# A four-layer cross-attention and expert kernel: first query weight in four transfers, idle products ahead, and two query products moved up

## The reference, cut to what matters

```
h = layernorm(x)                                    # 1024 tokens x 512
# layer 0: 32 query heads of 128, 4 key/value heads; keys from context and h (128 per sequence)
q = h @ Wq0;  k, v = concat(ctx, h) @ Wk0, Wv0
x = x + softmax(q k^T / sqrt(128)) v @ Wo0
x = x + experts0(layernorm(x))                      # dense 512x512 + top 2 of 28 low-rank experts
# layer 1: 32 query heads of 128, 8 key/value heads; keys from the context alone (64 per sequence)
q = rmsnorm(h @ Wq1.T);  k = rmsnorm(ctx @ Wk1.T);  v = ctx @ Wv1.T
x = x + softmax(q k^T / sqrt(128) + mask) v @ Wo1.T
x = x + experts1(layernorm(x))                      # top 2 of 8
# layers 2 and 3: another attention, experts, and a clustered linear part; untouched here
```

## Time and profile before

| | |
|---|---|
| median of three runs | 1587.48 us |
| the profiled execution's own time | 1586.25 us |
| span in the trace, first to last instruction | 1584.4 us |
| TensorE (PE) busy | 1502.9 us, 95% |
| VectorE (DVE) busy | 1010.4 us, 64% |
| ScalarE (ACT) busy | 820.3 us, 52% |
| GpSimd (POOL) busy | 380.0 us, 24% |
| mean granted TensorE clock | 0.984 |

### The profile page before, as it was taken

The page is one execution under the profiler, slowest core; times in us unless marked ns, Lnnn a source line. Parts: engine busy times, 40 slices in busy tenths (PEclk is TensorE's granted clock), DMA queues, the critical chain, the costliest instruction groups (busy, mean ns, idle before and its releaser), DMA issues.

```text
span 1584.4 us, 27734 instructions
## 1 busy us (share of the span) xinstructions
PE 1502.9 (95%) x9626; PEld 1321.7 (83%) x9626; DVE 1010.4 (64%) x2475; ACT 820.3 (52%) x2862; POOL 380.0 (24%) x388
## 2 busy tenths in 40 slices
PE   6999999999999998989999999999999998779996
PEld 5899999999999987778888888888888887667775
DVE  6556556655665568765566656666565677688775
ACT  4455445645555455346565655555555652464542
POOL 4102010210111011133232323323232321543420
PEclk9999999999999999999999999999999998899998
DMA  5100100100011001010101010101010001111001
GB/s 182 59 28 28 41 28 28 58 10 28 28 54 41 28 13 41 28 40 28 41 28 41 28 41 28 50 19 67 3 66 32 5 8 54 43 49 40 21 14 57
DMA packets 14191, 60.21 MB, mean 38 GB/s; under 512 B 2036, under 2 KB 3444, under 8 KB 8936
## 3 DMA queue, kind: packets, MB, share of 16 engines
q1 hardware_dynamic: 14056, 58.46, 10.4%
HBM read 56.36 MB, written 2.10 MB: 37 GB/s over the span
## 4 chain that ended last, share of the span: by engine, by line
PE 58%; issue 27%; DVE 8%; POOL 4%; ACT 2%; DMA 0%; POOLq 0%; DVEq 0%; SPq 0%; ACTq 0%
PE psY L865 15%; PE psQ L786 10%; PE psKV L808 8%; PE psSO L755 3%; PE psSO L852 2%; PE psQ L771 2%; PE psTP L818 2%; PE psSO L756 2%; PE psTP L771 1%; POOL wo L483 1%; PE psTP L836 1%; POOL wkv L483 1%; PE psQ L716 1%; PE psKV L729 1%; PE psQ L1130 1%
## 5 line engine op out<-in xcount | busy, mean ns | idle before, releaser
L865 PE MATMUL psY<-wo,oT 128*128 128x512 f32 x1536 | 384.9, 399 | 1.8 <-DVE oT L1699 1.2
L865 PEld LDWEIGHTS psY<-wo,oT 128*128 128x128 f32 x1536 | 278.4, 188 | 66.0 <-POOL wo L483 2.2
L483 POOL TENSOR_TENSOR wo<-stage_o,wo 128x512 fp32r<-128x512 f32 (+2 forms) x71 | 91.3, 1316 | 323.0 <-ACT wo L1261 323.0
L1261 ACT ACTIVATE pT<-psTP 128x512 fp32r<-128x512 f32 (+1 forms) x128 | 62.9, 491 | 168.3 <-PE psTP L836 168.3
L589 POOL TENSOR_TENSOR rms<-ms_eps,minus_half 128x5 f32<-128x5 f32 x64 | 74.7, 1167 | 284.7 <-DVE ms_eps L1862 283.9
L1335 ACT ACTIVATE prob<-s_sb,neg_mx 128x64 f32<-128x64 f32 x256 | 86.0, 337 | 104.9 <-DVE neg_mx L1849 104.9
L1338 ACT ACTIVATE prob<-wide,neg_mx 128x128 f32<-128x128 f32 x256 | 99.8, 391 | 73.9 <-DVE neg_mx L1849 73.7
L1699 DVE TENSOR_TENSOR pT<-psTP,pT 128x512 fp32r<-128x512 f32 (+1 forms) x128 | 71.2, 557 | 78.6 <-ACT pT L1261 77.7
L1699 DVE TENSOR_TENSOR v<-psKV,v 128x128 fp32r<-128x128 f32 x64 | 18.7, 292 | 147.1 <-ACT v L1261 147.1
L808 PEld LDWEIGHTS psKV<-wkv,arena 128*128 128x128 f32 x768 | 99.5, 190 | 12.8 <-issue 6.3
L771 PE MATMUL psQ<-hT,wq 128*128 128x256 f32 x768 | 101.5, 288 | 7.7 <-DVE hT L1699 6.4
(11 more groups left out here) (296 smaller groups left out, 3377.2 us busy)
## 6 DMA issues: line engine op xcount, KB each, us to landing
stage_q<-in_wq SPq DMA_DIRECT2D x16, 1024.0 KB, 5.3
stage_o<-in_wo SPq DMA_DIRECT2D x16, 1024.0 KB, 4.8
stage_kv<-in_wkv SPq DMA_DIRECT2D x12, 512.0 KB, 3.6
stage_q<-in_ctx SPq DMA_DIRECT2D x16, 256.0 KB, 2.7
stage_o<-in_ctxT SPq DMA_DIRECT2D x2, 1024.0 KB, 7.3
stage_q<-in_base SPq DMA_DIRECT2D x2, 1024.0 KB, 5.8
out<-x_res SPq DMA_DIRECT2D x8, 256.0 KB, 2.3
x_res<-in_x SPq DMA_DIRECT2D x1, 1536.0 KB, 14.0
```

The lines of the kernel that those rows point to most:

```text
L483: g.tensor_tensor(dst[LO], stage, dst[HI].bitcast(f32), ALU.subtract).then_inc(ld[done or what + "_lo"], 1)
L865: m = mm(psY[:], oT[:, ol, h, :], wo[:, wl, h, :], start=h == 0 and i == 0, stop=h == HQ - 1 and i == 2)
L1261: copy = lambda o, i: nc.scalar.activation(o, i, ACT.Copy)
```

## The change

The first query weight comes in four transfers of 256 KB, each with its own semaphore (`slot0` to `slot3`, which also take over for the later context transfers); SP then waits for the second tile of x before it issues the context, the key weight and the rest. ScalarE and DVE take the slices as they come: three high slices, the tile 0, the fourth slice, tile 1. PE runs ten products of the identity with itself before the first transposes, one between them and five after them; nobody reads their result. In the first attention the high part of the first output weight moves from step 2 to step 1, behind the high part of step 1's keys, and POOL's low part of it moves behind the last `ln_rstd(0, n)`. In the second attention the query products of steps 1 and 2 are made whole at the end of steps 0 and 1, ahead of the query transposes there; that of step 1 is written to psY in place of psQ. `high_wkv` at the last step of a head group moves ahead of the exponentials and `oT_hi`.

```diff
@@ def of banks
+    def q_bank(st):
+        return psY if st.t == 1 else psQ
@@ sync
-        load_wq(io["wq0"][0], 0)
+        for k in range(KT):
+            sp.dma_start(stage_q[:, k], io["wq0"][0][:, k]).then_inc(ld[f"slot{k}"], 16)
+        sp.wait_ge(ld["x1"], 16)
         sp.dma_start(stage_o[:], io["ctxT"][0]).then_inc(ld["ctx_in"], 16)
@@ gpsimd
             if n == 5:
                 low_ctx(1)
-            if n == 6:
-                low_wo(0)
+        low_wo(0)
@@ tensor
             def q_proj(st, first, last):
-                if first == 0:
-                    need(pe, s["q_read"], st.t)
+                if first == 0 and st.t > 1:
+                    pe.wait_ge(s["q_read"], 1 if st.t == 2 else st.t)
...
-                        m = mm(by_eight(psQ[:]), lat(xl, k, n), wq_slice(st.div(NT) + a.wq0, wl, k),
+                        m = mm(by_eight(q_bank(st)[:]), lat(xl, k, n), wq_slice(st.div(NT) + a.wq0, wl, k),
...
                 if a.rms:
-                    if t.exists:
+                    if t.exists and t.t not in (1, 2):
                         q_proj(t, 0, 2)
                     if t2.exists:
                         p_transpose(t2)
                     if t.exists:
-                        q_proj(t, 2, 4)
+                        if t.t not in (1, 2):
+                            q_proj(t, 2, 4)
                         kv_proj(t)
...
                 if t.exists and a.rms:
+                    if t.t < 2:
+                        q_proj(t.back(-1), 0, 4)
                     q_transpose(t)
                     k_transpose(t)
...
+        def idle_products(count):
+            for _ in range(count):
+                mm(psKV[:, 0:P], ident[:], ident[:], start=True, stop=True)
+
         pe.wait_ge(setup["const"], 3)
-        for n in range(2):
-            ln_transpose(0, n, lambda: None)
+        idle_products(10)
+        ln_transpose(0, 0, lambda: None)
+        idle_products(1)
+        ln_transpose(0, 1, lambda: None)
+        idle_products(5)
@@ scalar, attention
                 if a.kv_new(t):
                     kv_read(t)
+                if a.rms and t.res(8) == 7 and t.exists:
+                    if t.static and t.t == STEPS - 1:
+                        high_wkv(13, 144)
+                    else:
+                        high_wkv(t.div(8) + 6)
...
-                if a.rms and t.res(8) == 7 and t.exists:
-                    act.wait_ge(s["kv"], a.kv_n(t) + 1)
-                    if t.static and t.t == STEPS - 1:
-                        high_wkv(13, 144)
-                    else:
-                        high_wkv(t.div(8) + 6)
+                if not a.rms and t.static and t.t == 1:
+                    kT_hi(t)
+                    high_wo(0)
...
-                if t.res(8) == 2 and not (t.static and t.t >= STEPS):
+                if t.res(8) == 2 and not (t.static and t.t >= STEPS) and (a.rms or t.t > 2):
...
-                    if a.kv_new(t):
+                    if a.kv_new(t) and (a.rms or t.t != 1):
                         kT_hi(t)
@@ scalar, start
-        high_wq(0)
+        for k in range(3):
+            first_wq(k)
         ln_hi(0, 0)
+        first_wq(3)
         ln_hi(0, 1)
@@ vector, start
-        low_wq(0)
+        low_wq(0, 2)
         ln_lo(0, 0)
+        low_wq(0, 3)
         ln_lo(0, 1)
         low_ctx(0)
```

More of the change, by code:

```diff
@@ L453, in _ @@
         for n in range(3):
-            sp.dma_start(stage_q[:, n], io["ctx"][:, n]).then_inc(ld[f"c{n}"], 16)
+            sp.dma_start(stage_q[:, n], io["ctx"][:, n]).then_inc(ld[f"slot{n}"], 16)
         sp.wait_ge(N3["w"], 1)
@@ L462, in _ @@
             sp.wait_ge(N3["f_lo"], n - 2)
-            sp.dma_start(stage_q[:, n % 3], io["ctx"][:, n]).then_inc(ld[f"c{n % 3}"], 16)
+            sp.dma_start(stage_q[:, n % 3], io["ctx"][:, n]).then_inc(ld[f"slot{n % 3}"], 16)
         sp.wait_ge(N3["q_tr"], NT)
@@ L1270, in high, with first_wq @@
             copy(dst, stage).then_inc(ld[what + "_hi"], 1)
+        def first_wq(k):
+            act.wait_ge(ld[f"slot{k}"], 16)
+            copy(wq[:, HI, k], stage_q[:, k]).then_inc(ld["wq_hi"], 1)
         def high_wq(load):
             for k in range(KT):
-                high("wq", wq[:, HI, k], stage_q[:, k], (load + 1) * 16)
+                high("wq", wq[:, HI, k], stage_q[:, k], load * 16)
         def high_wq1(load, k):
-            high("wq", wq_slice(load, HI, k), by_eight(stage_q[:, k]), (load + 1) * 16)
+            high("wq", wq_slice(load, HI, k), by_eight(stage_q[:, k]), load * 16)
         def high_wo(load, n=KT):
@@ L1502, in ctx_exp @@
         def ctx_exp(n):
-            act.wait_ge(ld[f"c{n % 4}"], (n // 4 + 1) * 16)
+            act.wait_ge(ld[f"slot{n % 4}"], (n // 4 + 2) * 16)
             nc.scalar.activation(wide[:], stage_q[:, n % 4], ACT.Square,
@@ L1711, in link, with low_wq @@
             dve.wait_ge(chain, mark(instruction))
-        def low_wq(load, stage=stage_q):
-            for k in range(2, KT):
+        def low_wq(load, *slices):
+            for k in slices or (2, 3):
                 dve.wait_ge(ld["wq_hi"], load * 4 + (k + 1))
-                sub_hi(wq[:, LO, k], stage[:, k], wq[:, HI, k]).then_inc(ld["wq_lo_v"], 1)
+                sub_hi(wq[:, LO, k], stage_q[:, k], wq[:, HI, k]).then_inc(ld["wq_lo_v"], 1)
         def ln_stats(ln, n):
@@ L1869, in qk_normalise @@
                 four = lambda t: t[:].rearrange("p (h c) -> p h c", h=HQ)
-                V.tensor_tensor(four(q_sb), four(psQ), rms[:, n, 0:HQ].unsqueeze(2).to_broadcast([P, HQ, HD]),
+                V.tensor_tensor(four(q_sb), four(q_bank(st)), rms[:, n, 0:HQ].unsqueeze(2).to_broadcast([P, HQ, HD]),
                                 ALU.mult).then_inc(s["q_read"], 1)
@@ L2057, in ctx_max @@
         def ctx_max(n):
-            dve.wait_ge(ld[f"c{n % 4}"], (n // 4 + 1) * 16)
+            dve.wait_ge(ld[f"slot{n % 4}"], (n // 4 + 2) * 16)
             V.tensor_reduce(small[:, 8 + n % 2:9 + n % 2], stage_q[:, n % 4], AX.X, ALU.max,
```

6 lines of the change are left out of this document (3 added, 3 removed).

## The result

The changed kernel takes 1570.69 us, the median of 4 runs (1569.39 to 1574.28); the kernel before took 1586.82 us beside it (4 runs, 1582.82 to 1587.54). The ratio is 0.9907, interval 0.9884 to 0.9931: about 15 us faster. The profiled execution took 1570.53 us with a span of 1568.7 us, against 1586.25 and 1584.4. So its own time fell by 15.7 us, where 10.5 were forecast.

What follows compares the result with a forecast made beforehand. TensorE, busy 95% of the span, was taken as the bound, through its waits and half-clock stretches after them. Terms 3.4 + 5.2 + 2.7 - 0.8 = 10.5 us off 1586.25 gave 1575.8 us; range 1569.5 to 1582.

Steps and rivals of the forecast that it cites:

- part 1: Last step of a head group: key weight split before the exponentials removes seven key-product waits, 3.4 us; bounds 0 and 3.4.
- part 2: Start of second attention: earlier query products bring the third query transpose 5.2 us sooner; bounds 1.9 and 6.9 us.
- part 4: Kernel start: first query product 3.2 us sooner, but 0.7 gained and 1.5 lost to clock, -0.8 us; bounds -3.5 and +1.2.
- part 3: First attention, output weight split a step earlier: 1.21 us wait and 1.51 us slow key product go, 2.7 us.
- I take the whole 3.4 us: Key weight split: all seven listed waits of 0.49 us counted as gain, 3.4 us, also the upper bound.
- so I let this loss stand: Second attention, after the third query transpose: half-clock loss of 1.7 us stays, because the wait ahead of it stays.
- The 1.2 that I gave for that case: Output weight split: if the clock falls nevertheless, only 1.2 us of gain is left.
- The landing of the rest of x: Kernel start: same bytes in the queue, so landing stays at 17.1 us; statistics start at best 1.2 us sooner.
- Rival 1: More half-clock stretches go: second attention's third 1.7, start's loss 1.5, later layers 1.7; 15.4 us gain, 1570.9 us; chance 0.15.
- Rival 2: Waits change place: low-keys waits lower the clock in second attention, start costs 3.5 us; 4.5 us gain, 1581.8 us; chance 0.16.
- rivals 3: Only the seven key-weight waits go, 3.4 us, other gains given back; 1582.9 us, within measurement; chance 0.09.
- rival 4: Slower: later layers drop the granted clock in new places; ten further losses make 17 us, 1592.8 us; chance 0.03.

Runs made afterwards that it cites:

- two other traces: Kernel before with one part each: output weight split a step earlier alone, 1582.69 us; start alone (four transfers, idle products, order of slices), 1586.91 us.
- The four kernels with single parts: Kernel before with one part each: key weight split sooner, ratio 0.9974; two query products moved up, 0.9967; output weight earlier, 0.998; start, 1.0008.
- six groups in the right places: Changed kernel plus idle products in six waits: before tiles 2 and 3, third hidden transpose, last layer's first attention step, three in the third layer; 1565.45 us.
- two in wrong ones: Changed kernel with 12 idle products before tiles 2 and 3, plus 7 in the first layer's attention and 9 before the second hidden transpose; 1575.45 us.
- the fifth trace: Kernel before with only the query products of steps 1 and 2 of the second attention moved up, first weight in one transfer; 1580.17 us.

## Why the prediction was right or wrong

The forecast, 1575.8 us, was 5.1 us too high; the direction and the range, 1569.5 to 1582, held. The 5.2 us of the profiled pair that the sum lacks are 1.6 in part 1, 1.5 in part 2, 1.0 in part 4 and 1.3 in stages that no part touches (1.7 less the 0.3 and 0.2 the other way), less 0.1 in part 3. Of these, the 1.3 and 1.0 of part 2's 1.5 are a matter of the execution, as the table shows; that they fell this way is luck. The forecast said 3.4 for part 1 and -0.8 for part 4, and these two were mis-sized.

**Part 1** was right in its mechanism. ScalarE's split came ahead of the exponentials, POOL started 0.08 us after the probabilities were ready (755.50 against 755.00 + 0.42), and all seven waits went. Mis-sized was the term "I take the whole 3.4 us", and its upper bound as well: it measured 5.0. The listed idle time of a wait is not its price. The busy column shows the rest: in this stage TensorE's idle time fell by 3.4 us (4.12 to 0.71), and its busy time by 1.6 (571.49 to 569.92) with no instruction less. The fall over the whole stage, 5.0 us, is measured from starts to starts; its split is less firm, since the profile models the ends of products. My reading of it, which no run isolates: a product that ends in a wait has its last result's way out (its drain) uncovered, and that is counted as busy. I had left the drain out where I worked with durations in part 2, and did not put it in here. The Trainium skill (TensorE: Matmul & The Clock Gate, Step-by-step: what each phase is for) says that the drain of one product lies beside the start of the next; the 0.17 us that the gap behind 768.25 has beyond its listed 0.49 (2.13 - 1.47 = 0.66) agree.

**Part 2** was right step by step. Shifted to the start of the stage before (690.85 - 686.38 = 4.47 us), the changed trace has query product 1 at 696.5 (forecast: 696.7), the key product at 700.9 (701.25), query product 2 at 703.2 (703.65), the third query transpose at 712.4 (712.9). The first wait for the low keys was 0.84 us and not 1.1; at the next key product TensorE waited 0.39 us for the probabilities ahead of it, and the low keys came within that. A third, 0.31 us in step 3, I had not listed. The gain to that transpose was 5.7 us for 5.2 forecast. The step "so I let this loss stand" failed in the pair of traces: behind the remaining wait of 1.71 us the clock stayed full, and another 1.0 us went. But it did so in the unchanged stage of two other traces too (32.79 and 32.78), with the same wait of 1.71 us. The third loss was a matter of the execution, and it was 1.0 us where I had priced it at 1.7. So was the first (1.5 us), which these two traces lack as well and which I had taken to be there in every execution. The edit is worth 4.2 to 6.7 us, and 5.2 is inside.

**Part 3** was right: 2.6 us for 2.7, 2.0 where the clock had not fallen. The 1.2 that I gave for that case was too low: it was the one listed wait, while of the 2.0 us 0.4 are busy time (27.93 to 27.50), as in part 1, and 1.6 idle time. The listed wait was again too low a price.

**Part 4** was right in what it is for: the first product at 11.99 (forecast 11.8), a wait of 3.82 us behind it ("4 us or more"), and a loss of 1.59 us in the second unit (1.5). Two of its inputs were off. The landing of the rest of x does not stay: issued 2.0 us later, it landed at 5.13 + 11.1 = 16.2, 0.9 us sooner. And DVE's context work started 2.0 us sooner (12.90 against 14.92), not 0.7. So the second unit started at 20.58, where I had written 22, and the part costs nothing in its stage, -0.2 us, where I had -0.8 as a loss. With one transfer and without SP's wait the landing was at 17.2 again; which of the two moved it was not tried. And one trace with the old start had it at 14.9, so a landing is not as fixed as I took it: with the same bytes and the same order it varied by 2.3 us. Of the 7.0 us that I read as the time until the first normalised tiles, 6.7 are that; 0.3 is a later wait, at 21.94.

**The rivals.** Rival 1 gives the measured time, 1570.9, but only two of its three terms came: the third loss of part 2, 1.0 us, and one in other layers, 1.3 net; the loss at the start stayed. The 1.6 us of part 1 were in no rival, so that rival 1's number is met by luck. Rival 2's price did not come: the low-key waits left the clock at 1.00. Nor did rivals 3 and 4, though what rival 4 builds on is real: in the last layers of one and the same kernel the clock falls in one execution where it stays in another, and they differ by 3.1 us.

**Open** is what decides which form the last layers take. The four kernels with single parts all show the longer one (226.1 to 226.5 us), the kernel before and one of two traces of the changed kernel the shorter. Where the difference lies is known, mostly behind the wait of 2.67 us in the last layer; why the clock falls there in one execution and not in the next is not. This could also be why the four single ratios multiply to less gain than the whole has; with one trace of each that is an argument and not shown.

## What to carry to other kernels

Price a wait at its listed idle time plus what the busy time of the stage loses with it: compare idle and busy of a window, not the list of waits alone (here 0.49 us listed, 0.71 real). Where waits pull TensorE's clock down, work moved up removes wait and loss together; idle products can only hold the clock, and only where they stand in the wait itself (5 us gained with six groups in the right places; two in wrong ones made their stages 3.3 us longer). And cut at least two traces of each kernel into stages before believing a stage's difference under 4 us; the landing of the first transfers needs the same care.

## What the runs showed of the hardware that was not expected

- Behind the same wait of 2.67 us the granted clock fell in one execution of a kernel and stayed in the next: 4.94 against 2.89 us for the same 12 products. Behind the wait of 1.71 us for q_sb it fell in two traces (before, key weight alone) and stayed in the three other parts alone and in both of the changed kernel.
- An idle product of 128 x 128 in 32 bits leaves two records; ten took 4.64 us at the very start and five 1.28 us a little later, so 0.46 and 0.26 us each.
- The same 1 MB transfer, issued at 1.71 or 1.72 us, was there at 9.5 to 9.7 us in four traces and at 7.24 in a fifth. Four transfers of 256 KB gave the first quarter at 6.12 us in the changed kernel, and the 1.5 MB queued behind them landed at 16.2, 0.9 us sooner than in the kernel before, though issued 2.0 us later; in the fifth trace, behind one transfer, they landed at 14.9.
- At the start the column of the granted clock is no guide: it shows 1.00 from 15.05 to 20.05 us in the kernel before, where 24 products take 5.00 us, and 24 like them take 3.12 us at 22.36. There the durations tell the level.
